# DLRM tower on one Trainium2 core: the last batch's layer blocks stand in other gaps, and the last tile's pairs are picked by two engines

## What is computed

```
e = jnp.stack([tbl_0[ids[:, 0]], ..., tbl_25[ids[:, 25]]], axis=1)
combined = jnp.concatenate([e, r_dense_x[:, None, :]], axis=1)      # 2048 x 27 x 128
interact = jnp.einsum('bfd,bgd->bfg', combined, combined)
z = interact[:, _TRIU_I, _TRIU_J]                                   # 351 pairs, i < j
h = jnp.concatenate([z, r_dense_x], axis=1)                         # 479 columns
h = jnp.maximum(h @ W_top1 + b_top1, 0.0)                           # 512
h = jnp.maximum(h @ W_top2 + b_top2, 0.0)                           # 256
y = h @ W_top3                                                      # 1
```

## Time and profile before

| what | us |
|---|---|
| median of 3 runs | 381.9 (381.5 to 384.46) |
| profiled execution | 383.58 |
| its span, first to last instruction | 381.8 |
| TensorE busy in it | 340.4 (89%) |
| GpSimd busy in it | 269.0 (70%) |
| VectorE, ScalarE busy in it | 235.5, 188.6 |

### The profile page before, as it was taken

The page is one execution under the profiler, slowest core; times in us unless marked ns, Lnnn a source line. Parts: engine busy times, 40 slices in busy tenths (PEclk is TensorE's granted clock), DMA queues, the critical chain, the costliest instruction groups (busy, mean ns, idle before and its releaser), DMA issues.

```text
span 381.8 us, 12053 instructions
## 1 busy us (share of the span) xinstructions
PE 340.4 (89%) x5340; PEld 245.6 (64%) x5340; DVE 235.5 (62%) x397; ACT 188.6 (49%) x283; POOL 269.0 (70%) x284
## 2 busy tenths in 40 slices
PE   4999898888996999599999999899996999799767
PEld 2677676666774655467677566667665455478666
DVE  6989999796998085369798567468963030303030
ACT  6678554555444353254445363554528246545413
POOL 7877777777777777777777777777777777777000
PEclk9999999999998999699999999999997899979879
DMA  7997233433343324324334323433221222222000
GB/s 188 260 263 218 70 86 93 100 82 86 90 102 80 80 57 97 92 59 101 71 102 95 96 58 76 114 84 80 55 56 52 56 54 54 57 53 55 16 4 0
DMA packets 24067, 33.34 MB, mean 87 GB/s; under 512 B 6463, under 2 KB 17473, under 8 KB 24016
## 3 DMA queue, kind: packets, MB, share of 16 engines
q0 software_dynamic: 8832, 18.11, 18.2%
q1 hardware_dynamic: 15184, 14.47, 16.2%
HBM read 32.55 MB, written 0.01 MB: 85 GB/s over the span
## 4 chain that ended last, share of the span: by engine, by line
PE 42%; POOL 38%; issue 15%; ACT 2%; DMA 1%; POOLq 0%; ACTq 0%
POOL gat L383 37%; PE prod L441 8%; PE prod L443 8%; PE gram L470 7%; PE back L512 6%; PE back L516 4%; PE front L415 4%; PE back L502 2%; DMA gat<-in_tbl,idx 1%; POOL oh_last L388 1%; ACT ct L626 1%; ACT h L651 1%; PE back L497 1%; PE gram L573 0%; PE prod L512 0%
## 5 line engine op out<-in xcount | busy, mean ns | idle before, releaser
L383 POOL DMA_INDIRECT gat<-in_tbl,idx x272 | 263.1, 967 | 83.1 <-issue 81.6
L739 DVE TENSOR_SCALAR ring<-idb,rowid 125x516 fp32r<-125x516 int32 x216 | 145.1, 742 | 9.8 <-PE prod L443 9.4
L441 PE MATMUL prod<-ring,tab_hi 125*128 125x512 f32 x272 | 112.0, 412 | 4.9 <-DVE ring L733 2.2
L443 PE MATMUL prod<-ring,tab_lo 125*128 125x512 f32 x272 | 108.3, 398 | 0.0
L746 DVE COPY z<-gram 128x216 f32<-128x216 f32 x32 | 12.2, 381 | 118.2 <-PE gram L470 118.2
L626 ACT COPY ct<-front 128x512 f32<-128x512 f32 (+2 forms) x80 | 72.0, 959 | 19.3 <-PE front L415 15.7
L470 PE MATMUL gram<-ct 128*32 128x27 f32 x4096 | 57.1, 196 | 12.2 <-issue 9.5
L470 PEld LDWEIGHTS gram<-ct 128*32 128x32 f32 x4096 | 47.3, 109 | 30.3 <-issue 26.4
L441 PEld LDWEIGHTS prod<-ring,tab_hi 125*128 125x128 f32 x272 | 51.8, 191 | 20.7 <-issue 5.3
L443 PEld LDWEIGHTS prod<-ring,tab_lo 125*128 125x128 f32 x272 | 52.0, 191 | 10.3
L415 PE MATMUL front<-ident,gat 128*128 128x128 f32 x272 | 43.6, 286 | 10.9 <-DMA gat<-in_tbl,idx 5.6
(11 more groups left out here) (73 smaller groups left out, 227.3 us busy)
## 6 DMA issues: line engine op xcount, KB each, us to landing
idb<-in_ids_t SPq DMA_DIRECT2D x27, 258.0 KB
gat<-in_tbl,idx POOLq DMA_INDIRECT x272
oh<-in_tbl SPq DMA_DIRECT2D x3, 448.0 KB
oh<-in_dense_t SPq DMA_DIRECT2D x4, 256.0 KB, 3.1
gat<-in_tbl SPq DMA_DIRECT2D x2, 448.0 KB
h<-in_tbl SPq DMA_DIRECT2D x2, 448.0 KB
w1z<-in_w SPq DMA_DIRECT2D x1, 702.0 KB
w2s<-in_w SPq DMA_DIRECT2D x1, 512.0 KB
```

The costliest lines, as they stand in the source:

```text
L383: nc.gpsimd.indirect_dma_start(out=gat[:, t % GS, i, :], out_offset=None, in_=tables[GATHERED[i]][:, :], in_offset=bass.IndirectOffsetOnAx ...
L441: nc.tensor.matmul(prod[:, :], tab_hi[0:OH_P, m, k, :], ring[0:OH_P, k, 0:SB], start=(k == 0), stop=False)
L443: nc.tensor.matmul(prod[:, :], tab_lo[0:OH_P, m, k, :], ring[0:OH_P, k, 0:SB], start=False, stop=(k == OH_K - 1)).then_inc(used, 1)
L739: nc.vector.tensor_scalar(ring[0:OH_P, k, :], idb[0:OH_P, n % IDB, :, 0:IW], rowid[0:OH_P, k:k + 1], None, ALU.is_equal).then_inc(built, 1)
```

## The change

Three things are done.

The order in the last batch is another. In tiles 12 to 14 the Gram steps `G` stand behind the chunks `T` with at most one layer block ahead of them, and the layer blocks J and N move: tile 12 takes four blocks of J and not three, tile 14 all seven of N; in tile 15 E[0] to E[5] all stand ahead of T[3], and E[6] comes at the very end. In batches 1 and 2 one block of J moves behind a one-hot product.

TensorE's stream has fewer waits: those for `gram_act`, `gram_dve` and `placed` at `G`, for `front_free` at the first two chunks of a tile, for `hi_ready`, and some before the layer blocks are gone, 57 instructions in all. In return SyncE's load of the dense rows now waits for the Gram products of a later tile.

For tile 15 the pairs are picked another way: VectorE turns `z1` in two parts, the low rows (13) first; ScalarE then wraps and picks the low part while VectorE turns and picks the other; the result goes to a free slot of `gat`. The three transposes go to three banks (`back`, `prod`, `gram`), and ScalarE, VectorE, ScalarE copy one each, every copy with a semaphore of its own for the layer block that needs it.

```diff
     if t == TILES - 1:
-        return T[0:1] + N[4:5] + T[1:2] + N[5:6] + T[2:3] + Z + T[3:4] + N[6:7] + E[0:3] + T[4:5] + E[3:4] + G + E[4:5]
+        return T[0:2] + Z + E[0:2] + T[2:3] + E[2:6] + T[3:5] + G
...
     if last and u == 0:
-        return T[0:4] + Z + T[4:5] + J[0:2] + G[0:1] + PL + G[1:2] + J[2:3] + G[2:4]
+        return T[0:4] + Z + T[4:5] + J[0:1] + G[0:1] + PL + G[1:2] + J[1:2] + G[2:4] + J[2:4]
     if last and u == 1:
-        return T[0:2] + J[3:4] + T[2:3] + Z + T[3:5] + J[4:5] + G[0:1] + PL + G[1:2] + J[5:6] + G[2:4]
+        return T[0:2] + Z + T[2:3] + J[4:5] + T[3:5] + G[0:1] + PL + G[1:2] + J[5:6] + G[2:4] + J[6:7]
     if last:
-        return T[0:2] + J[6:7] + T[2:3] + Z + T[3:5] + N[0:2] + G[0:1] + PL + G[1:2] + N[2:4] + G[2:4]
+        return T[0:2] + Z + N[0:2] + T[2:3] + N[2:4] + T[3:5] + N[4:5] + G[0:1] + PL + G[1:2] + N[5:6] + G[2:4] + N[6:7]
...
-END = [("Z", TILES - 1), ("L", NB, 2, 1), ("L", NB, 3, 0)]
+END = [("L", NB, 3, 0)]
...
                         sp.wait_ge(back_done, BACK_INDEX[("L", b - 1, 1, M1 - 1)] + 1)
+                        sp.wait_ge(gram_done, GC * (BT * b + 2))
                         sp.wait_ge(placed, BT * b)
                         load_dense(b + 1)
...
-                if TF * t + c >= 2:
+                if c >= 2:
+
                     pe.wait_ge(front_free, TF * t + c - 1)
...
                 if c == 0:
+
                     pe.wait_ge(front_free, TF * (t + 1))
-                    pe.wait_ge(placed, t + 1)
                     if t == 0:
+                        pe.wait_ge(placed, 1)
                         pe.wait_ge(pads_ready, 1)
-                if n >= 4:
-
-                    pe.wait_ge(gram_dve if c % 2 else gram_act, GC // 2 * (t - 1) + c // 2 + 1)
...
+            def turn_last_pairs():
+                pe.wait_ge(pairs_ready, TILES)
+                pe.wait_ge(low_picked, 1)
+                pe.wait_ge(back_free, BACK_INDEX[END[0]])
+                pe.wait_ge(prod_free, NP + len(PROD_INDEX))
+                for k in range(ZK):
+                    nc.tensor.transpose(third(k), zc_last[:, k * ZP:(k + 1) * ZP], ident[:, :]).then_inc(last_turned, 1)
...
-            turn_pairs(TILES - 1)
-            layer_step(*END[1][1:])
-            pe.wait_ge(back_free, BACK_INDEX[("Z", TILES - 1)] + 1)
+            turn_last_pairs()
             for m in range(M1):
                 layer_block(tail_banks[m], TAIL_JOB, 1, m).then_inc(tail_done, 1)
-            layer_step(*END[2][1:])
...
+
+            layer_step(*END[0][1:])
             for k in range(M2):
                 pe.wait_ge(tail_free, M1 + k + 1)
...
-            copy_pairs(TILES - 1)
-            finish_step(*END[1][1:])
+
+            act.wait_ge(low_turned, 1)
+            wrap(nc.scalar.copy).then_inc(low_wrapped, 1)
+            act.wait_ge(low_wrapped, 1)
+            nc.scalar.copy(zc_last[:, TOP * HALF:NPAIR].rearrange("p (g k) -> p g k", k=HALF), windows(z2, TOP, HALF)
+                           ).then_inc(low_picked, 1)
+            for k in (0, 2):
+                act.wait_ge(last_turned, k + 1)
+                nc.scalar.copy(zt[0:ZP, k, SB - P:SB], third(k)).then_inc(last_zt_act, 1)
...
+                nc.vector.transpose(z2[:, TOP:NF, 0:QUAD], z1[:, :, TOP:NF].rearrange("p g f -> p f g")).then_inc(low_turned, 1)
+                nc.vector.transpose(z2[:, 0:TOP, 0:QUAD], z1[:, :, 0:TOP].rearrange("p g f -> p f g")).then_inc(z1_turned, 1)
+                dve.wait_ge(z1_turned, TILES)
+                nc.vector.tensor_copy(zc_last[:, 0:TOP * HALF].rearrange("p (g k) -> p g k", k=HALF), windows(z2, 0, TOP)
+                                      ).then_inc(pairs_ready, 1)
+                dve.wait_ge(last_turned, 2)
+                nc.vector.tensor_copy(zt[0:ZP, 1, SB - P:SB], third(1)).then_inc(last_zt_dve, 1)
```

More of the change, by code:

```diff
@@ L106, in tile_steps @@
     if t == TILES - 1:
[L107 removed]
+        return T[0:2] + Z + E[0:2] + T[2:3] + E[2:6] + T[3:5] + G
     if last and u == 0:
[L111 removed]
+        return T[0:4] + Z + T[4:5] + J[0:1] + G[0:1] + PL + G[1:2] + J[1:2] + G[2:4] + J[2:4]
     if last and u == 1:
[L113 removed]
+        return T[0:2] + Z + T[2:3] + J[4:5] + T[3:5] + G[0:1] + PL + G[1:2] + J[5:6] + G[2:4] + J[6:7]
     if last:
[L115 removed]
+        return T[0:2] + Z + N[0:2] + T[2:3] + N[2:4] + T[3:5] + N[4:5] + G[0:1] + PL + G[1:2] + N[5:6] + G[2:4] + N[6:7]
     if u == 0:
[L117 removed]
+        return T[0:2] + O[0:1] + T[2:3] + Z + T[3:5] + O[1:2] + J[0:1] + G[0:1] + PL + G[1:2] + J[1:2] + G[2:4]
     if u == 1 and b == 0:
@@ L198, in build @@
         zc = z1_flat[:, 0:NPAIR]
+        zc_last = gat[:, (TILES - 2) % GS, 0:TCH, :].rearrange("p i d -> p (i d)")[:, 0:NPAIR]
         z2 = sb("z2", [P, NF, PITCH])
@@ L248, in build @@
         pairs_ready = sem("pairs_ready")
+        low_turned = sem("low_turned")
+        low_wrapped = sem("low_wrapped")
+        low_picked = sem("low_picked")
+        last_turned = sem("last_turned")
+        last_zt_act = sem("last_zt_act")
+        last_zt_dve = sem("last_zt_dve")
         back_done = sem("back_done")
@@ L308, in build, with third, wrap @@
         yrow = h1[0:1, 0, :]
+        def third(k):
+            return (back, prod, gram[:, 2, :])[k][0:ZP, 0:P]
+        def wrap(copy):
+            return copy(z2[:, TOP:NF, NF:PITCH], z2[:, TOP:NF, 0:HALF])
         block = ctx.enter_context(nc.Block())
@@ L478, in bank_clear, with last_back @@
                     pe.wait_ge(back_free, BACK_INDEX[step])
+            def last_back(job, n):
+                return max(BACK_INDEX.get(("L", job, n, m), 0) for m in range((M1, M2)[n - 1]))
             def inputs_ready(job, n):
@@ L485, in inputs_ready @@
                     return
-                for m in range((M1, M2)[n - 2]):
-                    step = ("L", job, n - 1, m)
-                    if step in PROD_INDEX:
-                        pe.wait_ge(prod_free, NP + PROD_INDEX[step] + 1)
-                    else:
-                        pe.wait_ge(back_free, BACK_INDEX[step] + 1)
+                pe.wait_ge(back_free, last_back(job, n - 1) + 1)
+                last = ("L", job, n - 1, (M1, M2)[n - 2] - 1)
+                if last in PROD_INDEX:
+                    pe.wait_ge(prod_free, NP + PROD_INDEX[last] + 1)
             def turn_pairs(t):
@@ L511, in layer_block @@
                     for k in range(ZK):
+                        if columns == TAIL_JOB and m == 0:
+                            pe.wait_ge((last_zt_act, last_zt_dve, last_zt_act)[k], (1, 1, 2)[k])
                         ins = nc.tensor.matmul(dst, w1z[0:ZP, k, units], zt[0:ZP, k, lo:hi],
@@ L528, in layer_step @@
                     pe.wait_ge(weights_in, 16 * 6)
-                bank_clear(("L", job, n, m))
                 if m == 0:
                     inputs_ready(job, n)
+                if m > 0 or n == 1 or BACK_INDEX[("L", job, n, m)] > last_back(job, n - 1) + 1:
+                    bank_clear(("L", job, n, m))
                 if beside(("L", job, n, m)):
@@ L754, in pick_pairs @@
                 dve.wait_ge(z1_turned, t + 1)
-                nc.vector.tensor_copy(z2[:, TOP:NF, NF:PITCH], z2[:, TOP:NF, 0:HALF]).then_inc(z2_wrapped, 1)
+                wrap(nc.vector.tensor_copy).then_inc(z2_wrapped, 1)
                 if t > 0:
@@ L761, in pick_pairs, with pick_last_pairs @@
                                       windows(z2, TOP, HALF)).then_inc(pairs_ready, 1)
+            def pick_last_pairs():
+                dve.wait_ge(gram_act, GC // 2 * TILES)
+                dve.wait_ge(gram_dve, GC // 2 * TILES)
+                dve.wait_ge(pairs_ready, TILES - 1)
+                nc.vector.transpose(z2[:, TOP:NF, 0:QUAD], z1[:, :, TOP:NF].rearrange("p g f -> p f g")).then_inc(low_turned, 1)
[5 more added lines that the diff above has]
+                nc.vector.tensor_copy(zt[0:ZP, 1, SB - P:SB], third(1)).then_inc(last_zt_dve, 1)
             dve.wait_ge(rowid_made, 1)
@@ L799, in _ @@
                     made += ahead_of(t)[c]
-            pick_pairs(TILES - 1)
+            pick_last_pairs()
 def windows(z2, row, n):
```

6 lines of the change are left out of this document (2 added, 4 removed).

## The result

The changed kernel takes 380.44 us (median of 10 runs, 377.3 to 384.97), the kernel before 382.99 on the same chip (10 runs, 381.5 to 384.46). The ratio is 0.9904, with a 95% interval of 0.9874 to 0.9934: about 1% faster (0.7% by the medians), where half a per cent slower was predicted. The time lies in the range, the sign is wrong. Medians and ranges are of all runs, but a ratio leaves out those over 1.5% above the fastest of their kernel, here two of the changed kernel's ten.

The account below looks back on a forecast made before the run. GpSimd's gathers were taken to bound the kernel until the last lands, then TensorE's 27.4 us chain. Terms +5.5 - 1.3 - 2.2 = +2.0 us on the median 381.9 gave 383.9 us, range 379.5 to 388.0.

Parts of the forecast that it names:

- What bounds the kernel: GpSimd's gathers up to the last one; behind it 27.4 us of TensorE's own chain, all the change can shorten.
- Start of the last Gram products, +5.5: Tile 15: with the new order they start at 367.5 us instead of 361.99, 5.5 us later.
- The walk up to tile 14: New block order timed with old durations: tile 14's last Gram product ends at 352.0 us, before 347.67.
- The pairs, "3.2 us": Tile 14: 3.2 us from the last Gram product to the last pick, ending at 355.2 us.
- The Gram products, -1.3: Last Gram products: shifted packet cuts leave one gap of 2.1 us, so 4.8 us instead of 6.1.
- The bound of -3.3: Best case for the last Gram products: no packet gap at all, 3.3 us saved.
- The end, -2.2: Behind the last Gram products: new pairs save 1.85 us, moving layer 3 of tile 14 saves 0.35.
- the -0.35 of layer 3: Last layers: layer 3 of tile 14 falls into the wait for its relu, saving 0.35 us.
- The sum: Whole kernel: +5.5 - 1.3 - 2.2 = +2.0 us, set against the median 381.9, giving 383.9 us.
- The clock stays full: Rival: no half clock at N[0], N[1], nor at E[0] to E[3]; 380.3 us, chance 0.22.
- The half clock reaches the last layers: Rival: half clock from the first `zt` part costs 1.5 us there, 0.9 in layer 2; 386.3 us, chance 0.25.
- The blocks fit: Rival: E[0] to E[5] done before tile 15's last gather, Gram products near 356.6; 373 us, chance 0.03.

Follow-up runs that it names:

- e5: Kernel before with 199 idle instructions at TensorE's start, cuts at rows 20 and 148; 391.72 us, ratio 1.024.
- e2: Changed kernel with the old pairs of tile 15; 379.96 us, ratio 0.9886.
- e3: Changed kernel with the old waits on TensorE; 386.18 us, ratio 0.9946.
- e4: Changed kernel with 23 idle instructions at TensorE's start, cuts back at rows 119 and 247; 382.39 us, ratio 0.9921.
- e6: Changed kernel with the last batch's old order and 33 idle instructions at TensorE's start, cuts at 3, 131 and 259; 380.07 us, ratio 0.993.
- e7: Changed kernel with E[4], E[5] behind the Gram products and idle instructions, cuts at 3, 131 and 259; 380.5 us, ratio 0.9894.
- e8: Changed kernel with old order in tiles 12 to 14, N[6], E[4], E[5] behind the Gram products, idle instructions; 380.01 us, ratio 0.9923.
- e14: Kernel before with only the fewer waits and later dense load, plus 56 idle instructions; 682.74 us where the kernel before took 674.08, ratio 1.0102.
- e10: Kernel before with only the fewer waits and later dense load, plus 56 idle instructions; 681.37 us where the kernel before took 674.35, ratio 1.0132.
- e1: Changed kernel with the last batch's old order, E[4] and E[5] behind the Gram products; 379.91 us, ratio 0.9897.
- e17: Kernel before with only the fewer waits and the later load of the dense rows; 380.32 us, ratio 0.9927.

## Why the prediction was wrong

*What bounds the kernel.* Right: the last gather ended at 354.13 us in the profile (before 354.11), no gather waited for TensorE for more than 0.3 us, and what differs between these two profiles lies behind it. It isn't so in the others: their last gathers ended at 352.4 to 353.6 (e5 aside), 0.5 to 1.8 us earlier. Their gathers were shorter, GpSimd being busy 267.3 to 268.5 us for 269.0; the pauses between them were the same. Whole spans of two profiles are therefore not to be set against each other without this.

*Start of the last Gram products, +5.5.* Measured +4.4. The walk up to tile 14 had N[0] and N[1] at the half clock; they ran at the full one, so the tile's last Gram product ended near 350.4 and not at 352.0, and E[0] began at 354.85 and not 356.6. Of that a part was given back, 11.5 us from E[0] to the Gram products for the 10.9 of the walk. The pairs, "3.2 us" from Gram product to pick, were as predicted.

*The Gram products, -1.3.* **This is the step that failed**: measured -3.7. The sum took one gap of 2.1 us, "the packet that begins with the fourth row is used up in 1.35 us and the next takes 3.45". The cuts were right, behind 3, 131 and 259. The gap at 131 did not come, the one at 259 did, and it fell where "VectorE is waited for anyway", as the sum had assumed for it. The bound of -3.3, no gap, was nearly the truth. I had made a rule, a packet takes 3.45 us, out of two gaps that follow directly on each other. The last cut in or just behind the Gram products bears it out roughly: in the twelve profiles that are not from the chips at 674 us the wait there was 1.36 to 2.57 us, and it ended 3.0 to 4.1 us behind the cut ahead (my estimate, from the rows of each piece). At the cut ahead of it, behind 102 to 131 rows, the wait was 0 in the changed kernel, e2, e3, e4 and e6, 0.32 in e7, 0.88 in e8, and 1.14 before; in e14 and e10, with the order of the kernel before and the cut one row on, it was 0.17 and 0.47. So neither the row of the cut nor the order fixes it.

The Trainium skill (Runtime: NRT & Kernel Launch, Instruction fetch mechanics) has the crossing from one block of 256 instructions to the next "mostly hidden". In this kernel it is not hidden at the last cut within the Gram products, 1.7 to 2.6 us a time, and it is where other work is waited for, as in the changed kernel.

*The end, -2.2.* Measured -2.6: 3.5 us to the first `zt` part for the 3.75 of the walk, and -0.5 for the -0.35 of layer 3. The mechanism was right. Yet e1 and e2 show that it isn't what makes the kernel faster: e1 has the old order, e2 the old pairs, and both are as fast.

*The sum.* Predicted +2.0, measured -1.95 in the profiles. The difference of 3.95 is 2.4 from the gaps, 1.1 from the start, 0.4 from the end, and 0.05 is left. That the forecast of 383.9 lies only 3.5 above 380.44 is luck: it was set on the median of three runs, 381.9, and the ten have 382.99; on that the same sum gives 385.0.

*The rivals.* "The clock stays full" gave 380.3 us, and 380.44 was measured, but by another road: half of it came true (N[0], N[1]; not E[0] to E[3]), and the missing gap did the rest. "The half clock reaches the last layers" did not come in this profile. It did in e2, e3 and e4. In e4 the clock was at half from 369.5 to 376.3, and its first 12 `zt` rows took 2.93 us for 1.60; all 24 took 5.3 for 2.8, so the half clock costs 2.5 there and not the 1.5 of the prediction:

```profile
370.97 2.93 PE L543 MATMUL front<-zt,w1z 117*128 117x128 f32 x12
```

The Trainium skill (TensorE: Matmul & The Clock Gate, Part 1) says that a change of the clock does not follow the kernel's start. The runs agree: the changed kernel's ten have mean clocks of 0.955 (384.97 us) to 0.982 (378.1), one program and one input. "The blocks fit" did not come.

What stays open: why the cut ahead of the last costs nothing in one kernel and 1.14 us in another; how much of e17's median gain of 2.5 us is the clock's, and whether it has that from the cuts; and why the gathers are shorter in some executions.

## What to carry to other kernels

In a long run of small matmuls, count the instructions, waits of their own included, and see where "issue" gaps stand in the trace: they come at a fixed count, and a few dozen instructions more or less anywhere ahead move them all. An edit that takes waits away can therefore gain (or lose) far from where it was made, and a new order that looks like the cause may be worth nothing; undo the parts one at a time before believing in it. A gap is best moved to where another engine is waited for, and its length should be given as a range from nothing up, not as a rule from one pair of gaps. And lay profiles beside each other from an event that they share, here the last gather, and write the granted clock beside each stretch: of the 6.0 us between the profiles of e17 and of the kernel before, 1.7 lie ahead of it, and 2.7 are the clock's.
